# Four fused layers on one core: six maxima of the attention layer in the last quad of layer 1, and a new order of its first projections and splits

## The reference, cut to what matters

```
xn = (x - mean) / sqrt(var + eps)           # per image and channel pair group
q, k, v = Wq xn + bq, Wk xn + bk, Wv xn + bv
s = q^T k ; e = exp(s/sqrt(8) - max(s/sqrt(8)))  ; out = (v e) / sum(e) ; x += Wo out + bo
```

## Time and profile before

| | us |
|---|---|
| median of the runs (lowest, highest) | 499.68 (498.82, 500.26) |
| the profiled execution | 501.63 |
| its span, first to last instruction | 499.8 |
| TensorE busy | 426.8 |
| VectorE busy | 348.5 |
| ScalarE busy | 277.9 |
| GpSimd busy | 126.4 |
| mean granted TensorE clock | 0.931 |

### The profile page before, as it was taken

One profiled execution on the slowest core, in us unless ns is written; L12 is line 12 of the kernel. 1 busy time (PEld: TensorE's weight loads), 2 busy tenths in 40 slices (PEclk: granted clock), 3 DMA queues, 4 the chain that ended last, 5 costly groups with the idle time before them and its releaser, 6 DMA issues.

```text
span 499.8 us, 9219 instructions
## 1 busy us (share of the span) xinstructions
PE 426.8 (85%) x3374; PEld 227.8 (46%) x3374; DVE 348.5 (70%) x688; ACT 277.9 (56%) x512; POOL 126.4 (25%) x163
## 2 busy tenths in 40 slices
PE   0525876899999998658998999998999999799997
PEld 0214756745555575223434343444534455355442
DVE  4638886522345677687998978979677687568785
ACT  1179984114035255324877877966287496476441
POOL 4330002200000002036653313124048066056000
PEclk9855998799999999695999999999999999889999
DMA  5400000550000043424430204405902832822500
GB/s 149 124 1 1 0 0 1 110 100 0 1 0 1 13 145 96 127 63 127 111 87 3 55 13 107 102 3 145 231 7 66 207 66 72 188 47 67 139 12 10
DMA packets 22090, 34.97 MB, mean 70 GB/s; under 512 B 5184, under 2 KB 18912, under 8 KB 20512
## 3 DMA queue, kind: packets, MB, share of 16 engines
q1 hardware_dynamic: 19696, 27.68, 22.2%
q0 software_dynamic: 1200, 5.44, 4.2%
q10 hardware_dynamic: 1152, 1.29, 1.2%
HBM read 16.78 MB, written 5.24 MB: 44 GB/s over the span
## 4 chain that ended last, share of the span: by engine, by line
PE 40%; DVE 9%; DMA 4%; POOL 2%; issue 2%; SPq 2%; ACT 1%; DVEq 0%; ACTq 0%; POOLq 0%
PE L_banks L1845 10%; PE L_banks L1745 7%; PE L_banks L1712 6%; PE L_banks L1819 5%; DVE L_mx L1323 3%; PE L_banks L1791 3%; DMA L_hats<-L_parts 2%; PE L_banks L1783 2%; DMA L_hat<-L_offsets 2%; SPq L1189 1%; PE L_banks L537 1%; PE L_banks L1725 1%; PE L_banks L1756 1%; PE L_banks L1767 1%; PE L_banks L1733 1%
## 5 line engine op out<-in xcount | busy, mean ns | idle before, releaser
L1323 DVE TENSOR_REDUCE L_mx<-L_banks 128x2 f32<-128x512 f32 x128 | 84.8, 687 | 20.5 <-PE L_banks L1712 19.5
L1460 DVE TENSOR_TENSOR L_s<-L_banks,L_cols 128x1024 f32<-128x1024 f32 x72 | 87.6, 1219 | 9.6 <-PE L_banks L1819 8.1
L1492 ACT ACTIVATE L_e<-L_banks 128x512 f32<-128x512 f32 x128 | 72.9, 597 | 30.2 <-PE L_banks L1725 24.9
L1845 PE MATMUL L_banks<-L_s,L_t_sb 128*64 128x256 f32 x576 | 79.4, 397 | 1.5 <-DVE L_s L1460 1.4
L1574 ACT ACTIVATE L_cols<-L_banks 128x512 f32<-128x512 f32 x72 | 42.8, 595 | 44.2 <-PE L_banks L1832 43.6
L1712 PE MATMUL L_banks<-stacks_k_st,stacks_q_st 64*128 64x256 bf16 x256 | 48.8, 293 | 6.3 <-DVE L_mx L1323 5.0
L1845 PEld LDWEIGHTS L_banks<-L_s,L_t_sb 128*64 128x64 f32 x576 | 35.4, 138 | 35.7 <-DVE L_s L1460 20.9
L1725 PE MATMUL L_banks<-stacks_q_st,stacks_k_st 64*128 64x256 bf16 x256 | 47.7, 284 | 1.4 <-ACT L_e L1492 1.4
L1819 PE MATMUL L_banks<-L_hats,L_sel 48*128 48x512 bf16 x144 | 43.8, 385 | 0.0
L1745 PE MATMUL L_banks<-L_e,L_v_x 128*32 128x256 f32 x512 | 41.9, 399 | 0.0
L1791 PE MATMUL L_banks<-all_w_all,L_xn 64*128 64x192 f32 x192 | 33.6, 346 | 3.3 <-ACT L_cols L1574 3.2
(11 more groups left out here) (286 smaller groups left out, 760.5 us busy)
## 6 DMA issues: line engine op xcount, KB each, us to landing
L_hat<-L_offsets SPq DMA_DIRECT2D x6, 576.0 KB, 6.3
L_hats<-L_parts SPq DMA_DIRECT2D x16, 216.0 KB, 9.4
L_stack<-L_xpad SPq DMA_DIRECT2D x12, 162.0 KB, 3.1
L_stack<-L_xpad SPq DMA_DIRECT2D x12, 153.0 KB, 3.7
L_mask<-L_masks SPq DMA_DIRECT2D x3, 576.0 KB, 9.4
L_hats<-L_parts SPq DMA_DIRECT2D x24, 72.0 KB, 3.0
L_hats<-L_parts SPq DMA_DIRECT2D x12, 144.0 KB, 3.1
L_q_parts<-L_parts SPq DMA_DIRECT2D x8, 192.0 KB, 2.9
```

Of the source, the lines that this page charges most:

```text
L1323: dve.tensor_reduce(mx[:, n % 2, :, head], ring[:, place["largest", step] % 3].rearrange("p (q s) -> p q s", q=2), AX.X, ALU.max).then_inc ...
L1460: dve.tensor_tensor(s[:, q], row_ps[:, q], cols[:, t % 3:t % 3 + 1].broadcast_to([P, 2, 2 * N]), ALU.mult).then_inc(prod_ready, 1)
L1492: act.activation(e[:, k], ring[:, 3 + v % 3], ACT.Exp, scale=HD2 ** -0.5).then_inc(e_ready, 1)
L1845: mm = pe.matmul(acc[C * half:C * half + C, b, 0:N], t_sb[:, b, h, (KK * half + t) * C:(KK * half + t + 1) * C], s[:, q, h, half * N:(half ...
```

## The change

- All splits are made by GpSimd alone, three operations each (subtraction, cast, subtraction); VectorE's `split` and GpSimd's `last_part` merge into one.
- In quad 2 ScalarE takes K's projection of group 0 only after the next quad's first SiLU, and the value products of group 0 move into quad 3, behind the mean; `take_values` of group 0 stands behind kv there, that of group 1 at the layer's end. The mean and spread of group 1 use another bank.
- SyncE stores and loads Q of group 0 before it stores and loads K.
- In quad 3 TensorE waits for group 0's stacks behind the output product and makes maxima 0 and 1, after the variance product maximum 2, after the value products maxima 3 to 5. VectorE takes them; the `bn_stats` of quads 2 and 3 move behind the last sum. The last preload of ScalarE's table goes, and the preload at the block's start.
- The centre product waits for each half of y on its own.
- The schedule of layers 2 and 3 begins at row -13. ScalarE writes the lines of groups 2 and 3 (rows -8 and -7 of its order). Projections stand at rows -5, -4, -2, -1, takes at -5, -4, 2 and 5, the value products at rows 7 and 10, all values in `a_ps`. Two filler products stand in each of the rows -13 to -6. `parts`, `full` and `rest` have buffers of their own, and ScalarE's wait for all parts at row 0 is gone; TensorE waits for the takes before rows 0, 1 and 6 instead.
- GpSimd's splits of group 2 stand behind image 1, those of group 3 behind image 2 and in front of image 3's copy; the loads of groups 2 and 3 behind images 3 to 6, six transfers each. SyncE stores group 2 behind image 2 and group 3 behind image 3.

The diff, cut to its core:

```diff
-    def split(self, dve, g, s, full, rest, parts):
...
+    def split(self, pool, g, s, full, rest, parts):
+        k = 2 * g + s
+        pool.wait_ge(self.hi_ready, k + 1)
+        if k:
+            pool.wait_ge(self.parts_ready, k)
+        pool.tensor_tensor(rest, full, parts[:, 0], ALU.subtract).then_inc(self.rest_ready, 1)
+        pool.wait_ge(self.rest_ready, k + 1)
+        pool.tensor_copy(parts[:, 1], rest).then_inc(self.mid_ready, 1)
+        pool.wait_ge(self.mid_ready, k + 1)
         pool.tensor_tensor(parts[:, 2], rest, parts[:, 1], ALU.subtract).then_inc(self.parts_ready, 1)
...
+LOADS = 6 + 6
+EARLY = 6
...
-                stacks.store_parts(sp, 0, parts[:, 0])
-                stacks.load_stacks(sp, 0, 0)
-                stacks.load_stacks(sp, 0, 1)
+                for s in range(2):
+                    stacks.store_parts(sp, 0, parts[:, 0], (s,))
+                    stacks.load_stacks(sp, 0, s)
...
+                    for step in range(2 if last else 0):
+                        stacks.take_largest(dve, step, early[step % 3])
                     dve.wait_ge(var_ready, q + 1)
                     dve.tensor_scalar(var[:], t_y[:, 0:2, :], EPS, None, ALU.add).then_inc(o_copied, 1)
                     if last:
                         add(q - 1)
+                        stacks.take_largest(dve, 2, early[2])
...
                 over_deviation(NQ - 1)
                 add(NQ - 1)
+                for q in range(NQ - 2, NQ):
+                    statistics(q)
+                stacks.take_values(dve, 1, b_v, bc_ps[:])
+                for step in range(3, EARLY):
+                    stacks.take_largest(dve, step, early[step % 3])
...
-                    pe.wait_ge(y_ready, 2 * q + 4)
                     for h in range(2):
+                        pe.wait_ge(y_ready, 2 * q + 3 + h)
                         mm = pe.matmul(t_y[:, 2 * h:2 * h + 2, :], center[:], y[:, 2 * h:2 * h + 2, :], start=True, stop=True)
...
                     if more:
                         conv_xs(q + 1, 8, 12)
+                    else:
+                        pe.wait_ge(acts_ready, 2 * q + 2)
+                        pe.wait_ge(stacks.stacked[0], LOADS * 16)
+                        for step in range(2):
+                            stacks.largest(pe, step, early[step])
...
-    LATE_LINES_AT = {-LAG + 5: (4, 5), -LAG + 6: (6, 7)}
-    PROJECT_AT = {-LAG + 7: 2, -LAG + 8: 3}
-    TAKE_AT = {-LAG + 8: 2, -LAG + 10: 3}
-    SPLIT_AT = {-LAG + 9: (2, 0), -LAG + 10: (2, 1), -LAG + 11: (3, 0), -LAG + 12: (3, 1)}
-    VALUES_PS_AT, VALUES_AT = {-LAG + 12: 2, -LAG + 13: 3}, {-LAG + 14: 2, -LAG + 15: 3}
+    LATE_LINES_AT = {FIRST + 5: 2, FIRST + 6: 3}
+    PROJECT_AT = {FIRST + 8: (2, 0), FIRST + 9: (2, 1), FIRST + 11: (3, 0), FIRST + 12: (3, 1)}
+    TAKE_AT = {FIRST + 8: (2, 0), FIRST + 9: (2, 1), 2: (3, 0), 5: (3, 1)}
+    VALUES_PS_AT, VALUES_AT = {7: 2, 10: 3}, {8: 2, 11: 3}
...
+                    if n == 3:
+                        stacks.split(pool, 3, 1, full[:, 1, 1], rest[:, 1], parts[:, 1, 1])
...
+                    if n == 1:
+                        for s_ in range(2):
+                            stacks.split(pool, 2, s_, full[:, 0, s_], rest[:, s_], parts[:, 0, s_])
+                    if n == 2:
+                        stacks.split(pool, 3, 0, full[:, 1, 0], rest[:, 0], parts[:, 1, 0])
+                    if n in (3, 4, 5, 6):
+                        stacks.load_stacks(pool, 2 + (n - 3) // 2, (n - 3) % 2)
...
-                    if v == 0:
-                        act.wait_ge(stacks.parts_ready, 2 * NQ)
...
+                    elif v < min(PROJECT_AT):
+                        keep_clock(pe, avg2, ring[:, 5], 2)
```

192 lines of the change are left out of this document (96 added, 96 removed).

## The result

The changed kernel takes **497.08 us** (median of 17 runs, 495.07 to 505.36), the kernel before 499.54 us in the same job: a ratio of 0.9949, 95% interval 0.9928 to 0.9970, so 0.5% faster. Forecast were 489.1 us, 2.1% faster, in a range that ended at 496.0. The direction was right, the time and the range were missed. In the five later jobs the kernel before had medians of 499.5 to 500.2 us.

The account below looks back on a forecast made before the run. Layer 2's front was taken as bound by VectorE and its turns with TensorE, a settled image by TensorE. Row 16 at 231.2 instead of 241.8 gave -10.6: 499.7 - 10.6 = 489.1 us on the median, range 486.0 to 496.0.

Parts of the forecast that it names:

- Quad 3's start: Layer 1: with the value products out of quad 2, quad 3 begins 1.9 us earlier, at 176.6.
- layer 1's tail: From K's projection to layer 2's block: sum +3.7 us, block at 202.9 instead of 199.2.
- the front: Layer 2's block start to first scores: shift at 209.6, four projections in 5.1 us, row 0 at about 216.0 against 226.97.
- Rows 0 to 7: Layer 2's first scores: ScalarE 7.3 us, TensorE about 6.5, VectorE 5.6; row 8 at 223.3 instead of 235.5.
- Rows 8 to 15: Layer 2: settled image 6.8 us plus second value products 1.1, so 7.9 where 6.3 stood; row 16 at 231.2.
- Behind row 16: Rest of the kernel: priced at nothing, the schedule untouched except transfers; what is won by row 16 stays won.
- The conversion to the median: Last term: the 10.6 us gain taken off the median, 499.7, as the profiled 501.63 us lay 1.95 above it.
- A: Clock falls in layer 2's new front: projections +3.7, rows 0 to 7 +1.9; gain 5.0, 494.7 us; chance 0.20.
- B: Longer layer 1 tail: stacks 2 us later, casts 1.16, VectorE waits out GpSimd; +3.5, 492.6 us; chance 0.10.
- C: Image 2's or 4's maxima come late, scores wait once or twice 1.5 us; 491.5 us; chance 0.07.
- D: As A, but clock stays at 1.2 GHz past row 8: 500.6 us until row 16, 506.6 until 24; chance 0.04.
- The early maxima: Six of 19 maxima moved from layer 2's front into layer 1; four enter the tail at 0.62 each, +2.5 us.

Follow-up runs that it names:

- second profile: The changed kernel unedited, run once more for its trace (one execution): 497.28 us, no ratio.
- profiled execution: The changed kernel unedited, the traced one of its first 17 runs: 505.36 us, at a mean granted clock of 0.935.
- e6: Changed kernel plus filler products before the stacks' wait and at layer 1's end, group 3's takes moved to rows -2 and -1: 492.4 us profiled, ratio 0.988.
- e17: Changed kernel with group 3's takes in the front and value products at rows 6 and 8 instead of 7 and 10: 491.4 us profiled, ratio 0.986.
- e8: The kernel before, unedited, run once more for a second profile: 501.3 us, no ratio.
- e15: Changed kernel with both halves of group 3 taken in the front instead of rows 2 and 5, nothing else: 495.8 us profiled, ratio 0.986.
- e5: Changed kernel plus filler products before the stacks' wait and at layer 1's end, scores of rows 0 to 7 multiplied twice: 493.6 us profiled, ratio 0.988.
- e7: Changed kernel without the six early maxima in layer 1, schedule beginning at row -19: 496.0 us profiled, ratio 0.991.
- the cover: Changed kernel plus ten filler products before group 0's stacks' wait, and 26 instead of 20 at layer 1's end: 499.5 us profiled, ratio 0.991.

## Why the prediction was wrong

**Quad 3's start, layer 1's tail, the front: right.** The second profile meets the forecast marks to 1.0 us up to the block, and the first scores came at 216.5 for 216.0. The wait for the stacks was 1.86 us for 1.2, since the o product ended 1.0 us earlier than I said (0.2 of it a slip: the prediction's own terms, 1.9 - 1.16 + 0.2, give 0.9 us and not the 0.7 that it used) while the stacks landed at 190.4, as forecast (190.7). In the profiled execution they landed at 191.1 and the wait was 3.04. The difference is on SyncE. Profiled execution:

```profile
176.16 5.22 SPq L591 DMA_DIRECT2D stacks_q_st<-L_q_parts  x6
181.43 1.27 SPq L582 DMA_DIRECT2D L_k_parts<-L_parts  x2
185.15 3.68 SPq L591 DMA_DIRECT2D stacks_k_st<-L_k_parts  x6
```

second profile:

```profile
176.59 3.68 SPq L591 DMA_DIRECT2D stacks_q_st<-L_q_parts  x6
180.32 1.80 SPq L582 DMA_DIRECT2D L_k_parts<-L_parts  x2
184.36 3.68 SPq L591 DMA_DIRECT2D stacks_k_st<-L_k_parts  x6
```

Six issues of Q's load take between 3.68 and 5.22 us, and K's store stands behind them. K's load starts at 184.4 in the second profile, near the 184.6 where I had put it, and at 185.2 in the profiled execution. There the o product also ended 0.4 us earlier, which makes the rest of the longer wait. The terms of the splits were right: the cast on GpSimd took 0.61 us (forecast 0.6), the subtractions 1.16, a split 3.07 (3.0). That the first scores are released by the projections was right too.

**Rows 0 to 7: the step that failed.** I added up each engine's work (ScalarE 7.3 us, TensorE 6.5) and took the larger, for row 8 at 223.3. It came at 226.2, 2.3 us more than the forecast distance from row 0. The 7.3 us is met by e6, 7.0 us, where the takes do not stand between exponents. In the changed kernel the first take stands ahead of three exponents for which TensorE waits, and the second ahead of the value products; the waits put the value products 1.1 us later than in e6, and the clock, low behind them, costs 1.5 more: values at 2.08 us, context at 1.01. A sum per engine is a lower bound; the order of one engine's queue had to be followed through the other's waits.

**Rows 8 to 15: a wait not seen.** Forecast 7.9 us, 8.8 in the second profile (226.2 to 235.0), 8.9 in e6. The 0.95 us is the new wait at row 13 for the last values. I had counted the value product at row 10 and not its addition on VectorE at row 11, behind two maxima. e17 removed it and got the time back.

**Behind row 16.** The second profile took 2.5 us more here than the first profile of the kernel before, and 1.5 more than e8. In both, in e8, e6 and e15 the last image's transpose comes 115.3 us after the first image's at row 16, to a tenth, so nothing of layer 2's schedule was touched. What follows took 142.7 us (before), 143.7 (e8), 143.6 (e6), 144.9 (e15) and 145.2 (second profile). The change edits nothing there. The four profiles of the changed kernel take 143.7 to 145.3 us for this part, and e5, in which it is the same, takes 142.4, less than either profile of the kernel before; so 1.6 us at least are the spread of executions, and I read all of it as that, which is not shown.

**The conversion to the median.** The two profiled executions of the kernel before took 501.6 and 501.3 us, 1.9 and 1.7 above the medians of their jobs, and I took the whole difference of marks off the median. The second profile lies within 0.2 us of its own median. This is the last term; in which stretch a median execution of the kernel before is shorter, no profile shows. From 489.2 us of forecast span to 495.5: start -0.4, the way to row 0 +0.9, rows +3.3, the end +2.5, which is 6.3; the other 1.9 us is this conversion, and the forecast time of 489.1 misses 497.3 by their sum. Of these the rows are the mechanism that I had wrong; without their 3.3 us the time would have been 494.0, inside the range, and the rest, 4.9 us, is mostly the end and this conversion.

**The rivals.** A, the clock falls in the new front (0.20, 494.7 us), was the nearest, and names the right mechanism. It is what the long executions show at a higher price: a front of 21.6 us against the 13.1 forecast, +8.5, where A gave +3.7 for the projections. A left out the fillers, which at 1.2 GHz hold TensorE 1.7 us a row for eight rows. In the execution near the median A's front does not happen and its rows do (9.2 us by its price, 9.6 measured for rows 0 to 7). "TensorE: Matmul & The Clock Gate", Part 1, of the Trainium skill says that lack of activity halves the clock. That agrees with the second profile, where behind TensorE's waits in the rows the clock was down (mean 0.58 from 222 to 226 us) and the values took 2.08 us for 1.16. Which of two executions of one kernel loses the clock in the front, no profile here decides. B and C did not occur: the casts were short, and no scores waited for maxima. For D, a clock low past row 8, the profiled execution has a piece (0.84 over its last 12.5 us to row 16), but its 505.4 us come from the front: its rows took 19.1 us for the second profile's 18.5. My chance for the forecast, 0.59, was too high, and the range ended only 1.3 us above A.

**The early maxima** were the largest error of understanding. I priced them into the tail (+2.5) and out of the front, and never compared the two: e7 shows that they sum to nothing.

## What to carry to other kernels

An operation put on a second engine "in its free time" must be placed so that nobody waits for what stands behind it: here one line that moves two takes out of the stretch in which TensorE follows ScalarE row by row shows in the ratio (0.986 for 0.992), where the six early maxima, the cover and the fillers, each by itself, do not. Fillers that keep TensorE's clock are a stake: at 1.2 GHz they cost 1.7 times as much (1.22 us for 0.71) and may become the bound, so price a stretch at the low clock before placing them. Where the profiled execution lies away from the median, profile the kernel a second time before its trace is believed.
